# Logit products of a routing stage on the 16 gate columns instead of 112 columns padded with zeros

## The reference

```python
x = _layernorm(h).reshape(-1, D)                 # 7872 tokens, D = 128
gate_logits = x @ gate_weight.T                  # 16 experts: 7872 x 16
top_vals, top_idx = jax.lax.top_k(gate_logits, 2)
routing_w = jax.nn.softmax(top_vals, axis=-1)
mask = any(top_idx == arange(16))                # which tokens an expert has
h_ = silu(einsum('td,efd->tef', x, w1))          # expert products, F = 512
h_mean = einsum('tef,te->ef', h_, mask) / counts # mean over an expert's tokens
y_mean = einsum('ef,edf->ed', h_mean, w2)
out = h + einsum('tk,tkd->td', routing_w, y_mean[top_idx])
```

## Time and profile before

| | us |
|---|---|
| median of 3 runs | 421.34 |
| lowest and highest | 420.61, 424.37 |
| span of the profiled execution | 501.4 |

### The profile page before, as it was taken

The page is one execution under the profiler, slowest core; times in us unless marked ns, Lnnn a source line. Parts: engine busy times, 40 slices in busy tenths (PEclk is TensorE's granted clock), DMA queues, the critical chain, the costliest instruction groups (busy, mean ns, idle before and its releaser), DMA issues.

```text
span 501.4 us, 7310 instructions
## 1 busy us (share of the span) xinstructions
PE 397.6 (79%) x1929; PEld 269.9 (54%) x1930; DVE 311.4 (62%) x827; ACT 218.1 (43%) x423; POOL 205.3 (41%) x231
## 2 busy tenths in 40 slices
PE   8999999998898987554591404589987877899984
PEld 7888888886898974423440101244433433344552
DVE  3598888888788999543530101577744543577884
ACT  3334555445232666536350101456644443567320
POOL 2011111115400998757467775400066666610510
PEclk9999999998998996756587556799999788999998
DMA  6206533322209350647312111100291111100029
GB/s 182 66 1 164 139 86 109 102 80 82 81 1 262 98 140 2 193 140 212 106 57 52 54 52 43 31 0 2 54 331 47 37 47 42 47 16 1 1 73 251
DMA packets 53020, 43.68 MB, mean 87 GB/s; under 512 B 20686, under 2 KB 45980, under 8 KB 52732
## 3 DMA queue, kind: packets, MB, share of 16 engines
q1 hardware_dynamic: 44276, 32.09, 22.3%
q0 software_dynamic: 4416, 9.05, 6.5%
q10 hardware_dynamic: 4296, 2.15, 1.6%
HBM read 34.86 MB, written 8.42 MB: 86 GB/s over the span
## 4 chain that ended last, share of the span: by engine, by line
PE 47%; DVE 19%; issue 12%; another core or an unknown queue 10%; ACT 6%; POOL 3%; DVEq 2%; ACTq 0%; POOLq 0%
PE P L662 16%; PE P L935 14%; PE P L867 6%; ACT P L1265 4%; DVE BIG L1712 3%; DVE H L1828 2%; PE P L905 2%; PE P L1062 2%; PE P L697 2%; PE P L655 1%; POOL XN L597 1%; DVE arena L1504 1%; POOL arena L594 1%; PE P L688 1%
## 5 line engine op out<-in xcount | busy, mean ns | idle before, releaser
L1712 DVE TENSOR_TENSOR BIG<-BIG,P 128x512 f32 x138 | 95.0, 688 | 115.9 <-issue 75.1
L935 PE MATMUL P<-w1T,arena 128*128 x276 | 142.4, 652 | 12.0 <-DVE BIG L1712 8.7
L935 PEld LDWEIGHTS P<-w1T,arena 128*128 128x128 f32 x276 | 52.6, 209 | 67.1 <-issue 66.4
L1254 ACT COPY arena<-P 128x384 f32<-128x384 f32 (+1 forms) x48 | 22.4, 467 | 119.6 <-remote 50.4
L1265 ACT ACTIVATE P<-P 128x512 f32<-128x512 f32 x138 | 72.8, 580 | 1.6 <-PE P L935 1.5
L614 POOL DMA_INDIRECT XN<-table,arena x60 | 58.1, 968 | 30.1 <-issue 18.1
L614 POOL DMA_INDIRECT arena<-table,arena x42 | 39.7, 946 | 57.9 <-PE P L935 40.8
L557 POOL TENSOR_TENSOR rs<-ve,mhalf 123x4 f32<-123x4 f32 x16 | 17.6, 1098 | 101.9 <-DVE ve L1356 101.9
L1103 ACT ACTIVATE arena<-P 128x492 f32<-128x492 f32 x48 | 27.9, 583 | 50.6 <-PE P L662 50.5
L614 POOL DMA_INDIRECT BIG<-table,arena x36 | 34.6, 960 | 24.7 <-remote 12.4
L905 PE MATMUL P<-ident,XN 128*128 128x128 f32 x60 | 11.4, 304 | 41.6 <-issue 35.3
(11 more groups left out here) (242 smaller groups left out, 639.7 us busy)
## 6 DMA issues: line engine op xcount, KB each, us to landing
arena<-kpad SPq DMA_DIRECT2D x16, 492.0 KB, 4.0
XN<-in_L_ffn_w SPq DMA_DIRECT2D x1, 4096.0 KB
arena<-in_x SPq DMA_DIRECT2D x16, 224.0 KB
table<-XN SPq DMA_DIRECT2D x4, 896.0 KB
BIG<-table SPq DMA_DIRECT2D x1, 2048.0 KB
out<-H SPq DMA_DIRECT2D x8, 224.0 KB
out<-H ACTq DMA_DIRECT2D x8, 224.0 KB
BIG<-table SPq DMA_DIRECT2D x1, 1024.0 KB
```

Source lines behind the costliest of these rows:

```text
L935: mm = nc.tensor.matmul(bank[:, :], stat, w1T[:, bass.ds(e * FF, FF)], start=True, stop=True)
L1254: nc.scalar.copy(GTs[:, bank, 0:count * SLOT], PT[:, 0:count * SLOT]).then_inc(GT_ready, 1)
L1712: v.tensor_tensor(at, at, bank[:, :], ALU.add).then_inc(esum_step, 1)
```

## The change

The product of each batch takes the 16 columns of the gate alone and writes 16 columns. Nothing else is different: order, semaphores, buffers and the number of instructions are as before, and the 96 zero columns of `gateT` are still set and never read. There are 64 such products, 128 matmul records.

```diff
                 pe.wait_ge(ring_read, n + 1)
                 bank, at = P[n // 4], (n % 4) * 64
                 for q in range(4):
-                    mm = nc.tensor.matmul(bank[0:T, at + q * E:at + q * E + WARM], x2T[:, n % 2, q], gateT[:, 0:WARM],
+                    mm = nc.tensor.matmul(bank[0:T, at + q * E:at + (q + 1) * E], x2T[:, n % 2, q], gateT[:, 0:E],
                                           start=True, stop=True)
                 mm.then_inc(logits_mm, 1)
```

## The result

The changed kernel took 435.53 us (median of 4 executions, 431.44 to 438.77), the kernel before 421.68 us (4 executions, 420.61 to 424.37). The ratio is 1.0245 (95% interval 1.0209 to 1.028), slower. This ratio leaves out the two executions of the changed kernel near 438.7 us, over 1.5% above its fastest, which the experiments show to be the change's own. Median to median it is +13.9 us.

A forecast was written before the change was run, and what follows sets the result against it. VectorE's and GpSimd's routing chain bounds the kernel, TensorE 0.3 us behind at `ranks(1)`. A low clock adds 16.6 + 2.1 = 18.7 us, of which 15 reach the end: 421.3 + 15 = 436 us, range 420 to 441.

The forecast's parts named there:

- The edit removes nothing from the path: Routing products on TensorE: weight loads set the pace, so narrower matmuls save 0 at an unchanged clock; at most 5 us.
- The clock falls, and doesn't come back: Routing's first part: with 16 columns too little flows through TensorE's array, so its clock stays at 1.2 GHz, +15 us.
- The likeliest case: Clock low through the routing's whole first part, from 160 to about 200 us: 436 us, chance 0.48.
- for a part only: Rival: clock low for only some rounds of the routing's first part, +4 to +10 us, typically 428 us; chance 0.23.
- +16.6 us at `ranks(1)` for the whole stage: With the clock low throughout, TensorE comes to `ranks(1)` at 199.3 instead of 182.74 us; a round takes 2.48 against 1.28.
- +2.1 us more up to the bits: From `ranks(1)` to `bit_transposes(0)`, TensorE takes 5.4 us at the low clock instead of 3.27.
- Of 18.7 us 15 reach the end: Behind the first list: all 18.7 us at most, 10.8 at least as ScalarE's 7.92 us wait may absorb some; middle 15.
- The sum made against a profile whose span was 80 us longer than the median: Profiled span 501.4 us against median 421.34; excess placed where experts wait for gathered tokens, so routing differences carry over.
- The rise at 204.4 as a sign that transposes count: At the w1 transposes: the clock rose after 17 transposes alone, so transposes may hold it up; 0.41 us of flow a round.
- the clock does as before: Rival: dense weight loads count as work, the clock rises at 163.5 us as before; 421.3 us within 0.5, chance 0.20.
- Loads keep their speed at the lower clock: Rival: loads in the routing's products keep 0.1075 us each at the low clock; about +5 us, 426 us, chance 0.05.
- Faster: Rival: TensorE's freed time lies on the path at `ranks(1)`; at most 5 us gained, likely under 1, 420 us, chance 0.04.

The follow-up runs named there:

- last eight wide: Changed kernel with 112 columns in steps 8 to 15, 16 before: four executions 421.6 to 423.9 us, seven 429.2 to 431.9, one 1208.53.
- the delayed kernel: Kernel before (112 columns) with 37 unused 128 x 128 fp32 products right ahead of `ranks(1)`: 429.43 us against 421.69.
- 112 columns repeated: Changed kernel with 112 moving columns again, the 16 gate columns seven times over instead of zeros: 421.04 us, ratio 1.0003 to the kernel before.

## Why the prediction was right

The forecast was 436 us and slower, the result 435.53. The range that went with it, 420 to 441, held the unchanged time too, so it is the steps that tell whether the forecast was sound:

- **The edit removes nothing from the path.** Right. At 2.4 GHz the eight products of a step still take 0.93 us of records, and where the clock stays up through the stage with 112 columns TensorE waits for VectorE at `ranks(1)` anyway. A little was mis-sized in the edit's favour: a round of 16 columns is 162.92 - 161.69 = 1.23 us at the high level where I kept 1.28, and 2.38 at the low level where I had 2.48. Loads still follow one another by 206 ns, as shown above. What is shorter is the way from the first product of a round to the first transposition, 1.52 us (180.96 to 182.48) against 1.63 us for a wide round at the low level (172.04 to 173.67, last eight wide). That fits a shorter last matmul; the prediction had named this tail, as 10 to 36 ns, and put it at nothing.
- **The clock falls, and doesn't come back.** Right, and the step on which all hangs. The likeliest case, low from the start of the stage to its end, got 0.48 and came in 7 of 10 executions (by their times and mean granted clocks; one of them is profiled and shows it). The case "for a part only" got 0.23 and came in 3 of 10, +8.5 to +10.7 us where I gave +4 to +10. It is also the case of the profile that stands above, so the stage's low clock begins at 168.7 there and not at 160.
- **+16.6 us at `ranks(1)` for the whole stage.** Mis-sized by 1.9: 14.7, because of the shorter rounds (14 of them at 0.1 us) and because the clock fell only within `logits(0)`, which took 1.25 us where I had 1.66.
- **+2.1 us more up to the bits.** 16.9 - 14.7 = 2.2.
- **Of 18.7 us 15 reach the end.** This share was wrong. With 7.8 us of delay and the clock up, 7.7 arrived by the medians, and in the table each row that is 2 us or more late at the bits has 1.0 to 1.1 of it at the end, the delayed kernel alone 0.8. The lower bound rested on ScalarE's wait of 7.92 us, and that wait belonged to the one execution that was profiled before: with 112 columns repeated ScalarE's longest wait between 203 and 233 us is 2.38 us. The true sum of the likeliest case is 16.9 with all of it arriving, 437.7, which is where seven executions lie. That 436 came so close is luck: the rounds that I had too long made up for half of the share that I took off, and the median of four, 435.53, stands between two groups where no execution lies.
- **The sum made against a profile whose span was 80 us longer than the median.** Harmless for the sum, since the stage lies in the same place in both, but the excess was only in part where I had put it. The first expert product stands at 252.03 before, 95.4 us behind line 872, and 82.9 us behind it with 112 columns repeated (span 420.0). So 12.5 of the 80 us lie ahead of the experts, in the stretch in which ScalarE waits 7.92 us, and the rest among the experts.
- **The rise at 204.4 as a sign that transposes count.** That reading leaves out what stands ahead of them, four products of 512 columns at 198.49. With 112 columns repeated the rise comes at 203.4, 2.0 us into the transposes. No run separates the two, and nothing in the sum hung on it.

Of the rivals, "the clock does as before" is refuted for 16 columns: in the two profiles PEld is full for 8.30 and for 35.55 of 36.70 us and the clock falls or stays down all the same. "Loads keep their speed at the lower clock" is refuted: the loads' median is 329 ns in the view of line 705 above, and 206 ns lie between two. The Trainium skill, "TensorE: Matmul & The Clock Gate", section on LDWEIGHTS, gives columns / 1.2 ns without regard to the clock. Taken at both levels that is an estimate of +5 us for the whole stage; the runs show +17. "Faster" didn't occur in any execution, the quickest of ten being 429.33.

Open: how often the upper group comes was counted on ten executions, not explained, and of each group one execution is profiled. The place of the clock's first fall moves from one execution to the next with the same program, and no experiment here controls it.

## What to carry to other kernels

Before a matmul is made narrower, see what sets its pace: if that is the weight load (here about 107 ns from one to the next at the high level with 112, 64 or 16 moving columns), the columns in its shadow are free, and taking them away gains nothing but can cost TensorE its clock, which slows the loads too. Price such a cost by the records at both levels in the same trace, and ask where TensorE's margin to the next engine is: 0.3 us here, so nearly every low round counted in full. If a program's times fall into two groups, look at the granted clock of a profile of each before taking the median for the effect.

## What was not expected of the hardware

- At 1.2 GHz a load of 123 fp32 columns follows the last by 206 ns with 16 moving columns as with 112, at 2.4 GHz by about 107: the load's pace goes with the granted clock.
- Dense loads did not hold the clock: it fell at 168.7 us after 8.30 us in which PEld was busy without a pause. With 64 columns it came back, but only after 10 us, where 112 columns took 3.3.
- A higher mean clock isn't a shorter time: with 0.954 to 0.964 instead of 0.934 to 0.948 the kernel was no faster. The clock was low again, 198.0 to 204.9, in TensorE's longest work behind the stage.
- One execution in 12 of one kernel ran at a mean granted clock of 0.311 and took 1208.53 us. Its cause isn't known.
